# An attention layer on one core: P times V for two steps at a time, and the side work spread anew over even and odd steps

## The reference

```python
xn = layer_norm(x, norm_w, norm_b)
q = (xn @ q_w + q_b).reshape(8, 512, 16, 16);  k = likewise;  v = (xn @ v_w + v_b) * mask, likewise
att = softmax(einsum('bnhl,bmhl->bnmh', q, k) + (1 - mask) * -1e6, axis=2)
y = einsum('bnmh,bmhl->bnhl', att, v).reshape(8, 512, 256)
scale, shift = split(silu(cond) @ emb_w + emb_b, 2)
h = layer_norm(y, sb_norm_w, sb_norm_b) * (1 + scale) + shift
return x + silu(h) @ out_w + out_b
```

## Time and profile before

| | us |
|---|---|
| median of 3 runs (533.2 to 534.14) | 533.97 |
| the profiled execution's own time | 533.38 |
| its span, first to last instruction | 531.7 |
| TensorE busy | 510.8 (96%) |
| VectorE busy | 414.4 (78%) |
| ScalarE busy | 351.0 (66%) |
| GpSimd busy | 225.4 (42%) |

### The profile page before, as it was taken

The page is one execution under the profiler, slowest core; times in us unless marked ns, Lnnn a source line. Parts: engine busy times, 40 slices in busy tenths (PEclk is TensorE's granted clock), DMA queues, the critical chain, the costliest instruction groups (busy, mean ns, idle before and its releaser), DMA issues.

```text
span 531.7 us, 10099 instructions
## 1 busy us (share of the span) xinstructions
PE 510.8 (96%) x2851; PEld 190.9 (36%) x2851; DVE 414.4 (78%) x661; ACT 351.0 (66%) x645; POOL 225.4 (42%) x270
## 2 busy tenths in 40 slices
PE   8899999999999999999999999999999999988987
PEld 3423333433343333433343333333334333422334
DVE  6796778787887878787897879787887877877525
ACT  2316776677767777677767777677766777666761
POOL 4384223654353534544445444445436444234011
PEclk9999999999999999999999999999999999999999
DMA  5345353423325343342325343342335333251011
GB/s 153 121 126 182 86 162 98 139 82 104 120 78 162 88 135 101 124 137 79 120 82 163 95 139 90 103 149 79 120 89 169 99 94 90 89 156 37 20 60 40
DMA packets 55098, 57.95 MB, mean 109 GB/s; under 512 B 12424, under 2 KB 42248, under 8 KB 55072
## 3 DMA queue, kind: packets, MB, share of 16 engines
q1 hardware_dynamic: 52464, 55.40, 34.6%
q10 hardware_dynamic: 2608, 2.24, 1.5%
HBM read 36.35 MB, written 21.00 MB: 108 GB/s over the span
## 4 chain that ended last, share of the span: by engine, by line
PE 76%; ACT 9%; issue 6%; DVE 4%; POOL 3%; DMA 1%; ACTq 0%; SPq 0%; POOLq 0%; DVEq 0%
PE pv_ps L571 21%; PE st_ps L555 19%; PE mx_ps L519 11%; PE job_ps L612 7%; ACT probs L711 6%; PE job_ps L634 5%; PE job_ps L621 5%; PE mx_ps L659 3%; DVE negmax L906 2%; PE mx_ps L532 2%; ACT h_tanh L761 1%; PE mx_ps L664 1%; DMA k_rows<-qk_dram 1%; PE job_ps L485 1%; DMA x_in<-in_x 1%
## 5 line engine op out<-in xcount | busy, mean ns | idle before, releaser
L906 DVE TENSOR_REDUCE negmax<-mx_ps 128x2 f32<-128x1024 f32 x256 | 303.1, 1220 | 87.2 <-PE mx_ps L519 86.3
L711 ACT ACTIVATE probs<-st_ps 128x512 f32<-128x512 f32 x502 | 273.4, 600 | 125.6 <-PE st_ps L555 125.3
L555 PE MATMUL st_ps<-q_rows,k_rows 115*128 115x512 bf16 x502 | 157.4, 383 | 5.3 <-ACT probs L711 2.3
L571 PE MATMUL pv_ps<-probs,v_rows 128*32 128x512 f32 x1024 | 136.4, 605 | 0.6 <-ACT probs L711 0.6
L519 PE MATMUL mx_ps<-k_rows,q_rows 51*128 51x512 bf16 x512 | 79.6, 382 | 1.9 <-DMA k_rows<-qk_dram 1.9
L1184 POOL TENSOR_TENSOR qk_parts<-qk_rest,qk_parts 128x512 bf16<-128x512 f32 x31 | 36.0, 1162 | 103.9 <-DVE qk_parts L980 103.9
L555 PEld LDWEIGHTS st_ps<-q_rows,k_rows 115*128 115x128 bf16 x502 | 38.8, 97 | 107.6 <-ACT probs L711 76.1
L1169 POOL TENSOR_TENSOR qk_parts<-qk_full,zero 128x512 bf16<-128x512 f32 x29 | 32.0, 1103 | 96.6 <-ACT qk_full L733 96.6
L612 PE MATMUL job_ps<-x_norm_t,w_qk 128*128 128x512 f32 x116 | 58.0, 592 | 0.0
L519 PEld LDWEIGHTS mx_ps<-k_rows,q_rows 51*128 51x128 bf16 x512 | 15.8, 94 | 110.9 <-issue 54.4
L1175 POOL TENSOR_TENSOR qk_rest<-qk_full,qk_parts 128x512 f32<-128x512 f32 x31 | 35.9, 1158 | 4.2 <-ACT qk_parts L725 2.0
(11 more groups left out here) (116 smaller groups left out, 402.8 us busy)
## 6 DMA issues: line engine op xcount, KB each, us to landing
qk_dram<-qk_parts SPq DMA_DIRECT2D x128, 128.0 KB
q_rows<-qk_dram SPq DMA_DIRECT2D x124, 96.0 KB, 2.6
k_rows<-qk_dram SPq DMA_DIRECT2D x124, 96.0 KB, 2.6
x_in<-in_x SPq DMA_DIRECT2D x16, 256.0 KB, 2.9
...
k_rows<-mask_dram SPq DMA_DIRECT2D x64, 6.0 KB
...
```

The lines of the kernel that those rows point to most:

```text
L555: pe.matmul(st_bank(b, t, h), k_rows[0:ROWS_ALL, g, h, c * P:(c + 1) * P], q_rows[0:ROWS_ALL, g, h, :], start=True, stop=True).then_inc(st ...
L571: mm = pe.matmul(pv_ps[VW * h:VW * (h + 1), :], v_rows[:, c, g * GH + h, :], probs[:, t % P_SLOTS, h, :], start=(c == 0), stop=(c == CH - ...
L711: act.activation(probs[:, t % P_SLOTS, h, :], st_bank(b, t, h), ACT.Exp).then_inc(exp_done, 1)
L906: dve.tensor_reduce(by_pair[:, :, j, c], mx_ps[j][:, :, :], AXIS_X, ALU.max, negate=True).then_inc(max_done, 1)
```

## The change

- pv is done for two steps in every second step: an even step does the pv of steps t - 2 and t - 1, an odd one none; in body 7 from step 11 on, and in the epilogue, it stays one for each step.
- Jobs come in quarters: three in an even step (MOST), one in the odd step behind it (END). proj is cut into quarters of 256 columns.
- Side turns stand in odd steps only (but one in body 7). The two xturns of a body are side turns now, the first of them one body earlier, in step 15. Every odd step of a middle body has one.
- proj 3 moves into the body before, steps 14 and 15; for batch 0 into the prologue. outp is done two bodies late instead of one, in steps 0 to 3. The embedding moves from body 0 to steps 0 to 3 of body 1.
- On VectorE the copies and h stand behind both maxima, the split of the maxima ahead of outp's sum. On ScalarE the tanh of h has a table of its own.
- GpSimd takes the norms of x ahead of `take_rest` of group 2. SyncE places the maxima ahead of the saves (behind them for group 3) and saves the output of batch b - 2 behind `spread` of group 3.
- TensorE and ScalarE write out one more of the last bodies, as the other engines do already.

```diff
+ALL, MOST, END = (0, 1, 2, 3), (0, 1, 2), (3,)
+A, Z = (0, 1), (2, 3)
 JOBS = {
-    0: ("proj", 3, 0, AZ), 1: ("xturn", 0, 1, AZ), 2: ("xturn", 1, 1, AZ),
-    3: ("proj", 0, 1, A), 4: ("proj", 0, 1, Z), 5: ("vproj", 0, 1, A), 6: ("vproj", 0, 1, Z),
-    7: ("proj", 1, 1, A), 8: ("proj", 1, 1, Z), 9: ("vproj", 1, 1, A), 10: ("vproj", 1, 1, Z),
-    11: ("proj", 2, 1, A), 12: ("proj", 2, 1, Z), 13: ("outp", 0, -1, A), 14: ("outp", 0, -1, Z),
-    15: ("outp", 1, -1, AZ),
+    0: ("outp", 0, -2, MOST), 1: ("outp", 0, -2, END), 2: ("outp", 1, -2, MOST), 3: ("outp", 1, -2, END),
+    4: ("proj", 0, 1, MOST), 5: ("proj", 0, 1, END), 6: ("vproj", 0, 1, MOST), 7: ("vproj", 0, 1, END),
+    8: ("proj", 1, 1, MOST), 9: ("proj", 1, 1, END), 10: ("vproj", 1, 1, MOST), 11: ("vproj", 1, 1, END),
+    12: ("proj", 2, 1, MOST), 13: ("proj", 2, 1, END), 14: ("proj", 3, 1, MOST), 15: ("proj", 3, 1, END),
 }
...
-SIDE = {1: ("yturn", 3, -1), 5: ("yturn", 0, 0), 7: ("hturn", 0, -1), 9: ("yturn", 1, 0),
-        11: ("hturn", 1, -1), 13: ("yturn", 2, 0)}
+FIRST_JOBS = {1: ("xturn", 0, 1, ALL), 2: ("xturn", 1, 1, ALL), 3: ("proj", 0, 1, ALL), 5: ("vproj", 0, 1, ALL),
+              6: ("proj", 1, 1, ALL), 7: ("vproj", 1, 1, ALL), 8: ("proj", 2, 1, ALL), 11: ("proj", 3, 1, ALL)}
+SIDE = {1: ("yturn", 3, -1), 3: ("xturn", 1, 1), 5: ("yturn", 0, 0), 7: ("hturn", 0, -1),
+        9: ("yturn", 1, 0), 11: ("hturn", 1, -1), 13: ("yturn", 2, 0), 15: ("xturn", 0, 2)}
+SIDE_OF_0 = {1: ("xturn", 0, 1), 3: ("xturn", 1, 1), 5: ("yturn", 0, 0), 9: ("yturn", 1, 0), 13: ("yturn", 2, 0),
+             15: ("xturn", 0, 2)}
+LAST_JOBS = {0: ("outp", 0, -2, MOST), 1: ("outp", 0, -2, END), 2: ("outp", 1, -2, MOST), 3: ("outp", 1, -2, END),
+             10: ("outp", 0, -1, A), 11: ("outp", 0, -1, Z), 12: ("outp", 1, -1, A), 13: ("outp", 1, -1, Z)}
+LAST_SIDE = {1: ("yturn", 3, -1), 5: ("yturn", 0, 0), 7: ("hturn", 0, -1), 8: ("hturn", 1, -1),
              9: ("yturn", 1, 0), 13: ("yturn", 2, 0)}
-LAST_LATE = {(1, 2): ("proj", 3, 0), (7, 2): ("hturn", 0, -1), (8, 2): ("hturn", 1, -1)}
+LAST_LATE = {(0, 2): ("proj", 3, 0), (9, 0): ("hturn", 0, -1), (9, 2): ("hturn", 1, -1)}
+TANH = {8: 7, 12: 11}
+LAST_TANH = {8: 7, 9: 8}
...
-LATE = {(1, 2): ("proj", 3, 0), (6, 1): ("proj", 0, 1), (8, 2): ("hturn", 0, -1), (10, 1): ("proj", 1, 1),
-        (12, 2): ("hturn", 1, -1), (14, 1): ("proj", 2, 1)}
+LATE = {(0, 2): ("proj", 3, 0), (6, 2): ("proj", 0, 1), (9, 2): ("hturn", 0, -1), (10, 2): ("proj", 1, 1),
+        (13, 2): ("hturn", 1, -1), (14, 2): ("proj", 2, 1)}
-X_STAT = {(10, 2): (0,), (11, 0): (1,), (11, 2): (2,), (12, 0): (3,), (13, 0): (4,)}
-Y_STAT = {(2, 2): (0,), (3, 0): (1,), (3, 2): (2,), (4, 0): (3, 4)}
+X_STAT = {(11, 2): (0, 1, 2), (12, 0): (3, 4)}
+Y_STAT = {(2, 2): (0,), (3, 2): (1, 2, 3), (4, 0): (4,)}
...
-EMBEDDING = {13: (0,), 14: (1, 2), 15: (3,)}
-EMBEDDING_LOADS = (0, 1, 2, 3, 5, 6, 7, 9, 10)
+EMBEDDING = {(1, 0): 0, (1, 1): 1, (1, 2): 2, (1, 3): 3}
+EMBEDDING_LOADS = (0, 2, 3, 4, 6, 8, 10, 12, 14)
...
+def pv_steps(b, t):

+    last = isinstance(b, int) and (b == B - 1 and t >= WIDE_STEP or b == B)
+    if last:
+        of = (t - 1,)
+    else:
+        of = (t - 2, t - 1) if t % 2 == 0 else ()
+    return [(b, k) if k >= 0 else (b - 1, k + STEPS) for k in of]
...
-                return {7: (xt_ready, 1), 8: (mask_col_ready, 1)}.get(t)
+                return {7: (xt_ready, 1), 8: (mask_col_ready, 1), 11: (v_plain_ready, 2)}.get(t)
...
-                    for k in halves:
-                        mm = pe.matmul(ps, w_qk[:, k, i, :], x_norm_t[:, k, :], start=(k == 0), stop=(k == KD - 1))
+                    for q in quarters:
+                        h, k = q // KD, q % KD
+                        mm = pe.matmul(ps[:, h * D:(h + 1) * D], w_qk[:, k, i, :], x_norm_t[:, k, h * D:(h + 1) * D],
+                                       start=(k == 0), stop=(k == KD - 1))
...
+                if isinstance(b, int) and (b, t - 1) in EMBEDDING:
+                    pe.wait_ge(setup_chain, 6 + EMBEDDING[b, t - 1] + 1)
...
-                if 1 in halves:
+                if 3 in quarters:
...
-                    pv_step(b, t)
+                    for of in pv_steps(b, t):
+                        pv_step(*of)
...
+            def tanh_of_h(b, t):
+                of = of_loop(b, {}, TANH, LAST_TANH)
+                if t not in of or not side_at(b, of[t]):
+                    return
+                _, i, d = side_at(b, of[t])
+                act.wait_ge(h_lin_ready, KD * d + i + 1)
+                act.activation(h_tanh[:, i, :], h_lin[:, i, :], ACT.Tanh).then_inc(h_tanh_ready, 1)
...
-                    read_side(b, t - 1, 1)
+                    tanh_of_h(b, t)
...
-                    read_job(b, t - 1)
+                    read_y(b, t - 1)
+                    split_max(b, t)
+                    read_out(b, t - 1)
                     late_job(b, t, 0)
                     stats_at(b, t, 0)
-                    split_max(b, t)
                     max_pair(b, t, 0)
                     late_job(b, t, 1)
                     stats_at(b, t, 1)
                     max_pair(b, t, 1)
                     late_job(b, t, 2)
                     stats_at(b, t, 2)
...
-                if not (isinstance(b, int) and b == -1):
-                    take_rest(b, 0, 1)
-                    take_part2(b, 0, 1)
                 if exists(b - 1):
                     wait(pool, h_lin_ready, KD * (b - 1))
                     if isinstance(b, int) and b == 1:
                         pool.wait_ge(setup_done, 1)
                     pool.tensor_copy(mod_now[:, :, :], mod_half[:, :, :, bass.ds(b - 1, 1)].rearrange("p a k b -> p a (k b)")
                                      ).then_inc(mod_ready, 1)
+                if not (isinstance(b, int) and b == -1):
+                    take_rest(b, 0, 1)
+                    take_part2(b, 0, 1)
...
                 values(b + 1, 0)
                 values(b + 1, 1)
+                if exists(b + 2) and not (isinstance(b, int) and b == -1):
+                    x_norms(b + 2, CH)
                 take_rest(b, 2, 1)
                 take_part2(b, 2, 1)
                 values(b + 1, 2)
-                if exists(b + 2):
-                    x_norms(b + 2, CH)
+                if isinstance(b, int) and b == -1:
+                    x_norms(1, CH)
...
+                if i != NG - 1:
+                    place_max(b, i)
                 if exists(d):
                     save(0, 0, part0_ready)
                     save(1, 0, part0_ready)
-                place_max(b, i)
-                if exists(d):
                     save(2, 1, part1_ready)
                     save(3, 2, part2_ready)
+                if i == NG - 1:
+                    place_max(b, i)
+                if exists(d):
                     if first and i == 0:
...
             def body(b):
+                spread(b, 3, 0)
+                if exists(b - 2) and not last_body(b):
+                    save_out(b - 2, 0)
+                    save_out(b - 2, 1)
                 if exists(b - 1):
                     wait_apart(sp, maskp_ready, out_ready, 2 * (b - 1))
                     sp.dma_start(x_res[:, :, :], batch_of(x_dram, b - 1)).then_inc(res_loaded, 16)
-                spread(b, 3, 0)
                 spread(b, 0, 1)
                 if exists(b + 2) and not (isinstance(b, int) and b == -1):
...
-                for i in range(2):
-                    if exists(b - 1):
-                        wait_apart(sp, maskp_ready, out_ready, 2 * (b - 1) + i + 1)
-                        sp.dma_start(batch_of(out_dram, b - 1)[:, 2 * i:2 * i + 2, :], out_sb[:, 2 * i:2 * i + 2, :]
-                                     ).then_inc(out_saved, 16)
+                if isinstance(b, int) and b >= B - 1:
+                    save_out(b - 1, 0)
+                    save_out(b - 1, 1)
```

More of the change, by code:

```diff
@@ L691, in body @@
                     last_rows()
-            run(pe, body)
+            run(pe, body, B - 2)
         @block.scalar
@@ L745, in read_job, with read_xturn, read_side @@
                              ).then_inc(v_plain_ready, 1)
-            def read_side(b, t, half):
-                if not side_at(b, t) or side_at(b, t)[0] != "hturn":
+            def read_xturn(ps, i, d):
+                act.wait_ge(turned["xturn"], KD * d + i + 1)
+                wait(act, turned["proj"], NG * d)
+                act.activation(x_norm_t[:, i, :], ps, ACT.Identity, bias=nb_col[:, i:i + 1],
+                               scale=nw_col[:, i:i + 1]).then_inc(xt_ready, 1)
+            def read_side(b, t):
+                if not side_at(b, t):
                     return
-                _, i, d = side_at(b, t)
-                if half == 0:
+                kind, i, d = side_at(b, t)
+                if kind == "xturn":
+                    read_xturn(mx_ps[0][:, 0, :], i, d)
+                elif kind == "hturn":
                     act.wait_ge(turned["hturn"], KD * d + i + 1)
```

81 lines of the change are left out of this document (37 added, 44 removed).

## The result

The changed kernel takes 541.96 us (median of 4 runs, 540.15 to 543.76) against 534.06 us: ratio 1.0155, 95% interval [1.0134, 1.0176]. It is slower, as forecast, and the time lies in the range, 2 us above the 540. The parts of the sum came out less well than the sum.

A forecast was written before the change was run, and what follows sets the result against it. TensorE, busy 96% of the span, was taken as the bound. Prologue 1.1, bodies 0 and 1 1.0, bodies 2 to 5 3.0, body 6 0.4, body 7 0.8: 6.3 us on 533.4, 539.7, forecast 540; range 533 to 546.

The forecast's parts named there:

- The pv pair: Even step: pv for two steps saves a switch; second pv costs 0.91 us (ends 0.86 and 1.10), gain 0.8 a body.
- Rival (c): Second pv step: exposed weight loads cost 0.1 us or twice that in 61 pairs; 546 to 552 us, chance 0.12.
- The odd step: Waits for an exponential (0.26 us) and for the side turn's maximum (0.14 after the job); 2.84 us in all.
- rival (a): Odd step: without the wait on L654 the side turn no longer ends it, 0.14 us less; 531.5 us, chance 0.15.
- A middle body: Bodies 2 to 5: 61.4 us against 60.66, 0.75 us more in each, 3.0 us together.
- (b): No change: second pv costs 0.86 us and the hand-over takes 1.79; 535 us and a little more, chance 0.08.
- Rival (d): Even steps: VectorE late with a copy, holding the odd step's mx_ps 0.1 to 0.2 us; 543 to 546, chance 0.10.
- Body 6: About 0.4 us more, as its last step has no turn.
- Body 0: ... 0.6 less in all: Body 0: embedding gone, 3.4 us less; exponential waits, one more xturn and odd-step waits added; 0.6 us less.
- Moved work: Work moved on ScalarE, VectorE, GpSimd and SyncE costs TensorE nothing; cover for VectorE's copies is 0.1 us thin.
- The prologue's +1.1: Prologue: proj 3 of batch 0 between two maxima starves VectorE; between 0 and 1.7 us, taken as 1.1 more.
- Body 1: Gains the embedding and has no outp; 1.6 us more.

The follow-up runs named there:

- four_none: Changed kernel with whole jobs in even steps and none in odd ones (bodies 0 to 6): 565.12 us (one run).
- quarter_first: cast_later with the odd step's quarter of the job ahead of its second st_ps pair: 544.97 us, ratio 1.0212 to the kernel before.
- cast_later: Changed kernel with VectorE's copy of proj 3 in body 0 back behind step 1's maxima: 539.48 us, ratio 1.0102 to the kernel before.
- proj3_back: cast_later with proj 3 of batch 0 moved from the prologue back into body 0: 536.36 us, ratio 1.0064 to the kernel before.
- after_again: Changed kernel unaltered, traced a second time: 541.63 us (one run).

## Why the prediction was right, and where it was not

**The pv pair.** Right in kind. The second pv costs 1.86 - 1.00 = 0.86 us, the lower of the two ends, not 0.91. The sum had "0.54 + 1.00 + 0.91 + 0.98 + 1.29 = 4.72 us" for an even step; it is 4.66. Rival (c), exposed weight loads, is refuted: the time to mx_ps is 1.86, not over 2.0. The rule that was cited for it, from the Trainium skill's page "TensorE: Matmul & The Clock Gate", Part 3, would put exposed loads between passes that share all rows; this trace disagrees, with passes 0.43 us apart, no further than the two matmuls of half a job, which take 0.86, and no run here shows an exposed load in that place.

**The odd step.** Right: both waits are there, the exponential's (members 0.49 apart) and the turn's, and four_none and quarter_first show that the turn's is the one that ends it. The two are close, though: the quarter that starts at 248.73 would end 0.43 us on, at 249.16, and the turn starts at 249.21. Without the wait on L654, rival (a), an odd step from step 5 on would by this estimate win 0.05 us and not 0.14; no run took that wait away. The 2.84 us hold in steps 1 and 3; from step 5 on it is 2.76 us, the turn starting 1.74 after mx_ps and not 1.82. Part of this is rival (a)'s remark that the hand-over is not always the same; what makes it shorter was not tried. It does not save all of 0.08 either: a following step with a turn of maxima takes 4.98, not 4.90, since that turn waits for the same VectorE.

**A middle body.** 61.36 forecast, 61.02 found. By its terms: four even steps without a turn of maxima -0.23, four with one +0.08, the odd steps -0.19 (five turns that come 0.08 earlier, and step 15, 0.21 over its 2.84). So a body costs 0.36 us and not 0.75: the terms that were mis-sized are the second pv, 0.05 us eight times in the sum, and the hand-over, 0.08 us five times, a remark of mine in (a) and (b) that I priced and did not take. The later turns of maxima and step 15 give back 0.3 and 0.2 us of these 0.8, with no term in the sum. Rival (d), the copy on VectorE, did not come, by as little as was forecast ("that cover is 0.1 us thin"). VectorE's timeline, step 15 of body 3, where mx_ps of the odd step starts at 285.53:

```profile
285.46 0.42 DVE L1020 CAST qk_parts<-qk_rest 128x512 bf16<-128x512 f32 x1
285.99 2.36 DVE L942 TENSOR_REDUCE negmax<-mx_ps 128x2 f32<-128x1024 f32 x2
```

The copy ends at 285.88, 0.11 us ahead of the maximum, which starts at its usual 0.46 after mx_ps.

**Body 6.** Forecast +0.4, found -0.36. Half of the miss is that of every body; the other half is its last step without a turn, 2.30 us against 3.05, where I had taken off 0.35 only.

**The ends.** Here one step of the prediction failed: "Body 0: ... 0.6 less in all" has no term for the copy of proj 3, which stands one step earlier than before, and "Moved work" asked only how long VectorE needs for its copies, not when GpSimd has their input ready. In body 0 the copy waits 2.48 us for GpSimd's rest, holds the turn of step 1 and so costs 3.5 us (62.50 against cast_later's 59.04, and 4.7 in the second trace), of which 1.05 are the pv pair at the lower clock. I had looked at each queue alone and had not followed GpSimd to VectorE to the turn. The moved norms of x and SyncE's order, which the prediction put at nothing, play no part in this: the norm ahead of the rest is the prologue's, which did not move. With the copy back, body 0 is 0.28 less than before, near the 0.6. The prologue's +1.1 is right: proj 3 costs 15.05 - 13.88 = 1.2 there (against proj3_back). Against before it shows as 15.05 - 14.31 = 0.7, as that execution stands 0.37 us for a DMA ahead of its first st_ps. The other 3.0 us of the +3.73 were not in the sum: the first mx_ps of this execution comes 1.5 later (24.91 against 23.43 us), and the way from there takes 1.5 more at a low clock. Neither came again in after_again. Body 1 is near (+1.28 for 1.6), body 7 half a microsecond over (+1.3 for 0.8); no run took them apart.

In sum, on the profiled executions: 6.3 forecast; 2.5 less in bodies 2 to 6, 6.1 more from the start to the end of body 1, 0.5 more in body 7; 10.4 found. The first trace of the changed kernel is of the slowest of its four executions, with some 3 us at the start that the second does not have; the second has 8.2, near the 7.9 between the medians. There the 2.5 us too many in the middle stand against 3.9 too few up to body 1: that the total lies only 2 us off is luck in part, two misses of opposite sign.
